# Spreading the quantised layer's feed-forward over three attention phases, with one PSUM bank for each kind of product

## What is computed

```python
def _attn(x, ctx, wq, wk, wv, wo, bo, dq, dk, dv, dw):
    q, k, v = heads(x @ wq), heads(ctx @ wk), heads(ctx @ wv)      # 16 heads of 16
    sim = einsum('bhid,bhjd->bhij', _fq(q, dq), _fq(k, dk)) * SCALE
    attn = softmax(sim)
    out = einsum('bhij,bhjd->bhid', _fq(attn, dw), _fq(v, dv))
    return merge(out) @ wo + bo
h1 = _ln(x);  x = _attn(h1, h1, ...) + x
h2 = _ln(x);  x = _attn(h2, context, ...) + x
h3 = _ln(x);  a, g = split(h3 @ ff_w1 + ff_b1)                     # 1024 each
x = a * gelu(g) @ ff_w2 + ff_b2 + x
```

## Time and profile before

| | us |
|---|---|
| median of 3 runs | 2039.99 (2035.96 to 2040.37) |
| the profiled execution | 2040.25 |
| its span, first to last instruction | 2038.5 |
| TensorE busy | 1818.9 (89%) |
| VectorE, ScalarE, GpSimd busy | 1246.9, 1073.4, 905.4 |
| mean granted clock of TensorE | 0.928 |

### The profile page before, as it was taken

How to read it: one execution, slowest core, us unless ns; L and a number is a source line. 1 busy time by engine, 2 the same in 40 slices (tenths; PEclk the granted TensorE clock), 3 DMA queues, 4 the chain that set the end, 5 groups by cost and what they waited for, 6 DMA issues and landing times.

```text
span 2038.5 us, 34807 instructions
## 1 busy us (share of the span) xinstructions
PE 1818.9 (89%) x12481; PEld 1349.7 (66%) x12481; DVE 1246.9 (61%) x2220; ACT 1073.4 (53%) x3142; POOL 905.4 (44%) x1209
## 2 busy tenths in 40 slices
PE   4787887889889889989999999999999999999997
PEld 3676775656656656656767767677676676766766
DVE  5888889564464464464475674766746547455471
ACT  1122223565575575575465565655655565655562
POOL 4445555563363364364253553535543334333340
PEclk8899998788878878868999999999999999999999
DMA  7200000000200000000000200000000000000000
GB/s 221 92 11 6 6 6 11 1 6 18 71 2 6 6 1 6 6 1 6 6 1 13 83 7 6 1 12 2 6 6 2 6 7 6 22 6 1 11 1 11
DMA packets 31073, 35.66 MB, mean 17 GB/s; under 512 B 3164, under 2 KB 29752, under 8 KB 30520
## 3 DMA queue, kind: packets, MB, share of 16 engines
q1 hardware_dynamic: 30904, 33.44, 5.2%
HBM read 31.34 MB, written 2.10 MB: 16 GB/s over the span
## 4 chain that ended last, share of the span: by engine, by line
PE 63%; DVE 16%; ACT 11%; issue 7%; POOL 3%; DMA 0%; SPq 0%; DVEq 0%; POOLq 0%; ACTq 0%
PE ps L594 35%; PE ps L806 6%; PE ps L744 6%; PE ps L816 5%; PE ps L850 4%; ACT work L983 3%; ACT work L990 3%; DVE work L1183 3%; PE ps L766 2%; PE ps L607 2%; DVE xn L1037 2%; DVE rowmax L1187 2%; PE ps L831 2%; POOL work L1376 2%; ACT hT L899 1%
## 5 line engine op out<-in xcount | busy, mean ns | idle before, releaser
L594 PE MATMUL ps<-hT,w_slot 128*128 128x256 f32 x1696 | 419.5, 402 | 40.2 <-ACT hid L947 23.1
L594 PEld LDWEIGHTS ps<-hT,w_slot 128*128 128x128 f32 x1696 | 328.8, 200 | 104.4 <-ACT hid L947 28.5
L1300 POOL TENSOR_TENSOR work<-KT,own_head 128x512 f32<-128x512 f32 x256 | 262.5, 1047 | 285.3 <-PE ps L806 179.9
L990 ACT ACTIVATE work<-work,rowmax 128x128 f32<-128x128 f32 x768 | 245.1, 392 | 167.9 <-DVE rowmax L1187 167.1
L816 PEld LDWEIGHTS ps<-ident,work 128*128 128x128 f32 x1536 | 199.9, 153 | 170.2 <-issue 90.8
L983 ACT ACTIVATE work<-ps,rowmax,score_scale 128x128 f32<-128x128 f32 x512 | 229.3, 486 | 116.9 <-DVE rowmax L1191 116.2
L816 PE MATMUL ps<-ident,work 128*128 128x128 f32 x1536 | 266.7, 302 | 17.7 <-ACT work L990 17.0
L806 PE MATMUL ps<-work,QT 128*128 128x512 f32 x512 | 266.5, 605 | 9.9 <-POOL work L1300 4.9
L1376 POOL TENSOR_SCALAR work<-work,winv 128x128 f32<-128x128 f32 x512 | 185.0, 382 | 165.9 <-DVE winv L1203 163.5
L1217 DVE RECIPROCAL O<-ps 128x128 f32<-128x128 f32 x128 | 122.2, 955 | 174.5 <-PE ps L850 173.8
L976 ACT ACTIVATE work<-ps 128x512 f32<-128x512 f32 x256 | 150.6, 595 | 91.5 <-PE ps L816 91.1
(11 more groups left out here) (131 smaller groups left out, 3202.5 us busy)
## 6 DMA issues: line engine op xcount, KB each, us to landing
ctx_in<-in_ctx SPq DMA_DIRECT2D x32, 256.0 KB, 2.8
w_slot<-in_L_xattn_W SPq DMA_DIRECT2D x2, 1024.0 KB, 6.3
w_slot<-in_L_xattn_ff_w SPq DMA_DIRECT2D x1, 2048.0 KB, 11.4
w_slot<-in_L_xattn_ffn_w SPq DMA_DIRECT2D x2, 1024.0 KB, 8.8
w_slot<-in_L_xattn_w SPq DMA_DIRECT2D x2, 1024.0 KB, 10.1
out<-x_all SPq DMA_DIRECT2D x8, 256.0 KB, 2.1
x_all<-in_x SPq DMA_DIRECT2D x1, 1536.0 KB, 11.6
pad<-in_mask_Bx1x1xS_fk SPq DMA_DIRECT2D x1, 1024.0 KB, 7.6
```

The source lines that it names most:

```text
L594: mm = pe.matmul(dst, lhsT(k), rhs(k), start=(k == 0 and not onto), stop=(k == chunks - 1 and not more))
L990: ex = act.activation(prob[i % NPF][:, tok(h)], src[:, tok(h)], ACT.Exp, bias=shifts[:, at:at + 1])
L1300: pool.tensor_tensor(KB[u % NK].rearrange("p (h k) -> p h k", h=HU), keys, own_head[:, e:HC:2].unsqueeze(2).broadcast_to([P, HU, S]), ALU. ...
```

## The change

In layer 1 a new `spread_pass` takes the place of `joined_pass`. A stream's feed-forward is no longer beside one phase: f0 to f3 come at slots 8 to 11 of the phase in which its chain (ot, y, sum, norm, scale, tin) runs, f4 to f7 at slots 8 to 11 of the next, and y2 in four parts at slots 0 to 3 of the one after, its sum at slot 4. The next group's ctx, tin, k, q, v and keys of the stream move from behind y2 to slots 3 to 9 of the first of these phases, its norm and scale to slots 8 and 10 of the phase before. For this its transposed input goes to `O` (`hT_ahead`) and `hT` stays with the feed-forward. All `f` products and y2 use bank `one`, each waiting for the hid of the one before; ctx, tin, k, q, v and y use bank `other`, q waiting for the quantised k and v for the quantised q. The last fourth phase of the layer and the first of layer 2 keep the old joined order, with what is left of y2 at slots 0 and 1. No operation is added or taken away but ACT_TABLE_LOADs, which go from 30 to 42 in the program.

The core of the diff:

```diff
+SPREAD_START = {"tin": 3, "ctx": 4, "bias": 4, "k": 7, "q": 8, "v": 9, "keys": 9}
+SPREAD_NORM = {"norm": 8, "scale": 10}
+SPREAD_CLOSING = {"ot": 0, "y": 1, "sum": 1, "norm": 2, "scale": 4, "tin": 6, "bias": 8}
+SPREAD_HIDDEN = 8
+SPREAD_SUM = 4
+def spread_closing(layer):
+    pieces = PLAN[layer][-1]
+    y2 = [piece for piece, _, _, _ in pieces].index("y2")
+    chain = [(SPREAD_CLOSING[piece], piece, arg, n) for piece, _, arg, n in pieces[:y2] if piece[0] != "f"]
+    hidden = [(SPREAD_HIDDEN + int(piece[1:]) % (FC // 2), piece, arg, n) for piece, _, arg, n in pieces[:y2] if piece[0] == "f"]
+    product = [(part, f"y2{part}", pieces[y2][2], pieces[y2][3]) for part in range(Y2)]
+    product.append((SPREAD_SUM,) + pieces[y2 + 1][0:1] + pieces[y2 + 1][2:])
+    return chain, hidden[:FC // 2], hidden[FC // 2:], product
...
+            def spread_pass(layer, g, after, left):
+                into_a, into_b, into_c = left
...
+                attend(layer, g, 1, 0, middle(0) + into_a)
+                if after[0] != layer:
+                    attend(layer, g, 0, 1, middle(1) + into_b)
+                    pieces, later = joined(layer, g, after, 0)
+                    attend(layer, g, 1, 1, [(p[0] // 2 if p[2] != "sum" else 1,) + p[1:] for p in into_c] + pieces)
+                    pieces, _ = joined(layer, g, after, 1)
+                    attend(*after, 0, 0, pieces + later)
+                    return []
+                attend(layer, g, 0, 1, middle(1) + start(0, SPREAD_NORM) + into_b)
+                chain_0, first_0, second_0, product_0 = end(0)
+                attend(layer, g, 1, 1, chain_0 + start(0, SPREAD_START) + first_0 + start(1, SPREAD_NORM) + into_c)
+                chain_1, first_1, second_1, product_1 = end(1)
+                attend(*after, 0, 0, chain_1 + start(1, SPREAD_START) + second_0)
+                return product_0 + first_1, second_1, product_1
...
+                    if spread and piece == "ctx":
+                        pe.wait_ge(q["hT_ready"], C * due("tin", layer, g, 1))
...
+                    elif spread and piece in ("k", "q", "v"):
...
+                            pe.wait_ge(q["k_ready" if piece == "q" else "q_ready"], C * (use("att", layer, g, n["att"]) + 1))
...
+                    elif spread and piece[0] == "f":
...
+                        if f == 0:
+                            pe.wait_ge(q["hT_ready"], C * due("tin", layer, g, n["tin"]))
+                            if g + st:
+
+                                pe.wait_ge(c[1 - st]["yadd_done"], G * use("yadd", layer, g + st, 1))
+                        else:
+
+                            pe.wait_ge(q["hid_ready"], FC * use("ffn", layer, g, n["ffn"]) + f)
```

## The result

| | before | changed |
|---|---|---|
| median, us | 2039.85 (18 runs, 2035.28 to 2042.12) | 2043.66 (18 runs, 2040.45 to 2052.41) |
| ratio | | 1.0026, 95% interval 1.0017 to 1.0036 |
| profiled execution, span | 2040.25, 2038.5 | 2045.00, 2043.3 |
| mean granted clock | 0.928 | 0.943 |

The account below looks back on a forecast made before the run. ScalarE's exponentials bound a phase's first part, TensorE's packed products its second. The 13 phases (per group P0 long, P1, P2 short, P3 long) summed to 507.4 against 528.2, plus 2.0 ahead: -18.8, so 2021.5 us, range 2002 to 2048.

Parts of the forecast that it names:

- Part 2's walk: First part of a phase: y2's quarters behind scores 0 to 3 cost 1.5 us instead of 7.1.
- Part 5: tin and ctx ahead in long phases: one hT pair enters ScalarE's first part, 0.7 us; k finds hT ready.
- Part 3: Second part of a phase: products sharing one bank wait for its reader, 1.6 us, plus 0.5 at the phase's end.
- Rival 1: Three bare hand-overs in one bank come 0.9 us later each: 32 us, 2053.5; chance 0.22, shared with two other rivals together.
- The boundary: Phase end: VectorE's hid and OT stand ahead of the next phase's first maximum, 0.5 us (bounds 0 and 1.1).
- The base of the sum: The phase lengths were built up from one short phase's 27.5 us, giving 36.7 with gate products and waits.
- rival 3: Products spread more evenly keep TensorE's clock up: about 1.5 us a phase, 20 us more, 2001.5; chance 0.13.
- the gate products' move: Packed second parts: long phases lose four products, short ones get four, 7.1 us each; the move itself worth nothing.
- the waits for V at the boundary: After a long phase, the next waited 1.32 us for V before its second score; moving k, q, v earlier removes it.
- the table loads: Phase boundary on ScalarE: 12 more loads of 1.28 us each, the one back hidden by 0.7 us.
- a whole y2 in the last P3: The layer's last long phase stays at 49.8 us and gets y2 in two slots: 5.5 (3.4 to 7.1), 55.3.
- the two signs of being wrong: Hand-overs costing over 3 us a phase, or the first part of phases with y2 growing by more than 4.

Follow-up runs that it names:

- the norm's experiment: The changed kernel with the next group's norm and scale at slots 4 and 6 instead of 8 and 10; 2052.27 us, ratio 1.0066.
- both together: The changed kernel with two banks for products and gates, tin in the gate products' bank, y2's quarters at slots 1, 2, 3, 5; 1996.94 us, ratio 0.9815.

## Why the prediction was wrong

**The step that failed most is Part 2's walk: 1.5 us a phase for y2's place, where 3.8 were measured, five times.** It put score 4 at 10.5 us (11.2 measured), then jumped to k, "ending 0.6 later than now", and took 1.5 us. It did not follow ScalarE from the delayed score 1 through units 4 to 7: score 7 waits 1.68 us and k starts at 19.8, not at 18.2. It also reasoned that "products do raise the clock", where k ran at half (3.68 us), 8.5 us after the last quarter. The cost is 3.1 to 4.6 us in P1 and P3 (y2 packed against spread), and 3.5 of it goes when the quarters start a slot later (y2 later); the order rows of the change had shown the first quarter ahead of y.

**Part 5 had a wrong clause.** "k finds its hT long ready" is true of the data and false of the bank. k's bank holds the feed-forward's tin until ScalarE has copied it; k waits up to 1.86 us in P3 for such a copy, and ctx, which the sum did not price apart, 0.76 to 1.62 us. I had listed "one bank for each" as waits of q and f only, and not gone through every pair of neighbours in the bank. Worth 7 us (the edit with tin in `one`).

**Part 3's terms were mis-sized, not wrong.** q's wait is up to 1.07 us (1.0 forecast), 0.45 to 0.67 in some P1, P2 and P3. f0, turn and values cover v, as said. f to f is 0.31 and 0.32 in P0 and P1 (0.6 forecast together), but 0.95 and 0.32 in P2 and P3. There the hid stands behind V's quantising, in VectorE's timeline of P2:

```profile
755.99 0.75 DVE L1106 TENSOR_SCALAR O<-ps,rdeltas 128x512 f32<-128x512 f32 x1 [0.71 <-PE ps L651]
756.78 1.00 DVE L1108 TENSOR_SCALAR O<-O 128x512 f32<-128x512 f32 x1
757.89 1.07 DVE L1112 TENSOR_SCALAR V<-O 128x512 bf16<-128x512 f32 x1
758.88 0.47 DVE L1189 SCALAR_TENSOR_TENSOR hid<-ps,vcols,gate 128x256 f32<-128x256 f32 x1
```

The two middle steps are 0.43 us without GpSimd beside them. Rival 1 had named this ("quantising ahead of a hid") at 0.9 us for each of three hand-overs; it came to 0.6 for one. All of Part 3 is 26 us against 21.

**The boundary, 0.5 us in Part 3, was low.** Each P0 and P2 has 0.82 us ahead of y for OT, 6.3 us in the stretch, and in P1 and P3 the first quarter of y2 waits 0.43 for hid. ScalarE has 0.51 us of idle at the first exponential but 2.10 at the third unit's.

**The base of the sum was low.** It started from a P2 of 27.5 us; the three P2 phases of the stretch took 27.5, 27.9 and 28.3. The mean would have put some 0.4 us more into each of twelve phases, an estimate of 5 us in all.

**The clock: rival 3 was half right.** The sum left TensorE's busy time as it was. It fell by 23.1 us. 507.4 - 468.0 = 39 us of idle time were forecast and 83 came. The 44 us between them are not all cost: where TensorE waits for another engine, a higher clock only turns busy time into idle time, and how much of the error the clock hid is not shown. The first parts of P0 and P2 did stay near half clock (0.56 to 0.64 in the 11.6 us that answer to the earlier trace rows), while those of P1 stood at 1.00.

**What held:** the gate products' move at no cost of its own fits P0 (37.1, 37.8 and 38.7 against 37.4), though no run tests it alone; the waits for V at the boundary are gone; the table loads are hidden; a whole y2 in the last P3 costs 6 us (55.9, against 49.5 where y2 is packed ahead of it); and packed it costs 7 to 8. Of the two signs of being wrong, the hand-overs stayed under 3 us a phase (26 us over 12), and the first part grew by less than 4 in P1 (k at 19.8 against 16.6) but by 5 in P3 (k at 21.7). The waits on banks, the starting phase and the clock all stood in the text, k's wait for the bank did not; costs of under 3 us a phase, all on one side, turned -19 us into +4.

## What to carry to other kernels

When pieces share a PSUM bank, write down every neighbouring pair in that bank and the engine that reads the first; data that is ready says nothing about the bank. When work is spread over the start of a phase whose bound is a chain on another engine, try leaving the first slot free until that engine has two units to work on: here four matmul groups that began at slot 0 instead of 1 cost 13 to 17 us of 2040. And walk such a chain to its last unit, not to its middle.

## What the runs showed of the hardware

**VectorE beside GpSimd.** The quantising step from SBUF to SBUF (128x512 fp32) takes 0.43 us alone, up to 1.48 us in the changed kernel where it overlaps GpSimd's TENSOR_TENSOR instructions (1.09 us each for `weigh`, 1.27 for the 128x512 fp32 ones), and 3.26 at worst in the norm's experiment. Beside GpSimd's TENSOR_SCALAR (the scaling by winv) it stays at 0.43 to 0.45. The step that reads PSUM stays at 0.75 us in all 48 cases. The Trainium skill, "SBUF — State Buffer", section "SBUF: two separate sides", says that VectorE and GpSimd share a port pair as an exclusive lock that is held for a whole instruction, and the steps of up to 1.48 us agree: they are no longer than one such instruction and the step itself. The row of 3.26 us goes further: the step began 0.06 us after GpSimd's three instructions did and ended 0.28 us after the third, not after one.

**The same code at two lengths.** In the kernel of "both together" two P0 phases with the same instructions, and 4.5 and 4.4 us in which TensorE wasn't busy, took 36.47 and 34.36 us:

```profile
487.09:523.56 36.47, 32.00 (x184) 22.46 (x181) 20.05 (x46) 26.01 (x84) 19.06 (x40) 0.81 0.37 123
628.12:662.48 34.36, 30.01 (x185) 21.10 (x182) 20.03 (x46) 26.02 (x84) 19.07 (x40) 0.85 0.03 9
```

Of the 2.1 us, 2.0 are TensorE's busy time (32.0 against 30.0), at a clock of 0.81 against 0.85: it matters on which instructions the half clock falls. The first of the two also has the layer's weight loads beside it (123 GB/s); a third P0 without them took 37.1 at 0.77. The short phase ahead of the stretch differed by 6.0 us between two kernels (y2 packed, above). So a single phase of one trace should not be compared more closely than 2 us, and 6 can be noise.
